# Stage 0 of a transformer layer in token order, with the low-rank products of four tiles at once and the transposes five steps ahead

## What is computed

```
h = layernorm(x)
q = h @ Wq + h @ q_A @ q_B          # rank 16; 16 heads of 128
k = h @ Wk + h @ k_A @ k_B          # 4 heads of 128
v = h @ Wv + h @ v_A @ v_B
q, k = rms_norm, rope, gain (q)
y = causal softmax(q k^T) v,  minus its projection on v
x = x + y @ Wproj + y @ p_A @ p_B
x = x + W_down(silu(W_up h2) * (W_gate h2)),  h2 = layernorm(x), all three weights quantised to -1, 0, 1
```

## Time and profile before

| | us |
|---|---|
| median of 3 runs | 3926.59 |
| the three runs | 3903.36, 3926.59, 4186.11 |
| the profiled execution | 3899.53 |
| its span (slowest core, core 7) | 3898.0 |
| spans of the 8 cores | 3880.8 to 3898.0 |
| PE busy in the span | 3681.1 (94%) |
| DVE, ACT, POOL busy | 1775.4, 930.6, 759.0 |

### The profile page before, as it was taken

One profiled execution on the slowest core, in us unless ns is written; L12 is line 12 of the kernel. 1 busy time (PEld: TensorE's weight loads), 2 busy tenths in 40 slices (PEclk: granted clock), 3 DMA queues, 4 the chain that ended last, 5 costly groups with the idle time before them and its releaser, 6 DMA issues.

```text
span 3898.0 us, 52480 instructions; the slowest of 8 cores (3880.8 to 3898.0 us)
## 1 busy us (share of the span) xinstructions
PE 3681.1 (94%) x19448; PEld 1779.3 (46%) x19448; DVE 1775.4 (46%) x2311; ACT 930.6 (24%) x1658; POOL 759.0 (19%) x900
## 2 busy tenths in 40 slices
PE   6888898948998999999999999999999999999999
PEld 4555554534333444444444444444444444444444
DVE  5667676744346333344433334433333443333343
ACT  4567576744111544200000000000100000101000
POOL 3456666555544000000000000000000000000000
PEclk9999999979999999999999999999999999999999
DMA  6577776696334876546422225632222663222364
GB/s 170 150 217 210 204 219 196 209 207 214 120 118 145 296 283 251 192 173 229 178 77 79 76 76 205 227 141 76 76 76 76 227 229 117 76 76 79 109 230 155
DMA packets 124093, 629.68 MB, mean 162 GB/s; under 512 B 13264, under 2 KB 13584, under 8 KB 73152
## 3 DMA queue, kind: packets, MB, share of 16 engines
q1 hardware_dynamic: 96960, 469.80, 35.1%
q0 software_dynamic: 26880, 156.48, 13.1%
HBM read 555.61 MB, written 92.27 MB: 166 GB/s over the span
## 4 chain that ended last, share of the span: by engine, by line
PE 80%; DMA 7%; DVE 5%; issue 3%; POOL 3%; ACT 1%; DVEq 0%; SPq 0%; POOLq 0%; ACTq 0%
PE accps L1373 67%; PE accps L1177 4%; PE gps L400 4%; DMA pw<-W_gate 3%; DMA pw<-W_up 1%; DMA wq<-Wqkv 1%; PE yps L805 1%; PE sps L772 1%; DVE slabB L1256 1%; DVE ss L440 1%; DVE c L868 1%; DMA yst<-xb 1%; POOL rab L856 1%; DVE pacc L204 1%; DVE slabB L1254 1%
## 5 line engine op out<-in xcount | busy, mean ns | idle before, releaser
L1373 PE MATMUL accps<-slabB,xreg 128*128 128x512 bf16 x8192 | 1775.8, 380 | 3.4 <-DVE slabB L1256 3.4
L1373 PEld LDWEIGHTS accps<-slabB,xreg 128*128 128x128 bf16 x8192 | 803.2, 98 | 975.8 <-issue 16.2
L1373 PE MATMUL accps<-slabA,xreg 128*128 128x512 bf16 x4096 | 884.7, 379 | 0.0
L1386 ACT ACTIVATE xreg<-accps,scl 128x512 f32<-128x512 f32 x256 | 175.6, 688 | 2047.1 <-PE accps L1373 2041.8
L1373 PEld LDWEIGHTS accps<-slabA,xreg 128*128 128x128 bf16 x4096 | 400.8, 98 | 483.3
L1341 DVE TENSOR_SCALAR xreg<-xreg,scl 128x2048 bf16<-128x2048 f32 x192 | 246.6, 1284 | 604.1 <-PE accps L1373 576.2
L1344 DVE SCALAR_TENSOR_TENSOR xreg<-xreg,scl 128x2048 bf16<-128x2048 f32 x192 | 453.1, 2360 | 20.4 <-DVE xreg L1341 0.5
L400 PE MATMUL gps<-wq,slabA 128*128 128x512 bf16 (+1 forms) x2048 | 417.1, 335 | 16.8 <-DMA wq<-Wqkv 14.5
L1400 DVE SCALAR_TENSOR_TENSOR xreg<-accps,scl,xreg 128x512 f32<-128x512 f32 x256 | 192.0, 750 | 471.2 <-PE accps L1373 471.2
L1390 DVE TENSOR_TENSOR slabA<-xreg,accps 128x512 bf16<-128x512 f32 x256 | 175.1, 686 | 504.3 <-PE accps L1373 503.9
L72 POOL DMA_DIRECT2D acc_scr<-xreg x48 | 35.5, 739 | 1559.7 <-DVE xreg L1400 1546.4
(11 more groups left out here) (165 smaller groups left out, 2251.6 us busy)
## 6 DMA issues: line engine op xcount, KB each, us to landing
xreg<-W_down SPq DMA_DIRECT2D x128, 1024.0 KB, 7.8
pw<-W_up SPq DMA_DIRECT2D x128, 512.0 KB, 5.4
pw<-W_gate SPq DMA_DIRECT2D x128, 512.0 KB, 5.5
xreg<-W_up SPq DMA_DIRECT2D x64, 1024.0 KB, 5.2
xreg<-W_gate SPq DMA_DIRECT2D x64, 1024.0 KB, 5.0
xreg<-acc_scr POOLq DMA_DIRECT2D x64, 1024.0 KB, 7.3
acc_scr<-xreg POOLq DMA_DIRECT2D x48, 1024.0 KB, 5.2
outT<-xreg POOLq DMA_DIRECT2D x16, 1024.0 KB, 5.2
```

The source lines that it names most:

```text
L1373: pan_tok[k][tc] = op("tensor", lambda e, tc=tc, dt=dt, mov=mov: e.matmul(bank(st_ + tc), tern[s][:, dt * 128:(dt + 1) * 128], mov, start= ...
L1386: evict[k][tc] = op("scalar", lambda e, tc=tc, cs=cs: e.activation(silu[:, cs], bank(st_ + tc), AF.Silu, scale=scl[:, 1:2]))
```

## The change

Stage 0 takes the tiles in the order 0, 1, 2, ..., 15. Attention and the later groups keep the order TO; `unit_number` gives the place of a unit in either. The low-rank product is made for four tiles at once: `ln_lowrank(b)` in the steps 4, 8, 12 and 16, with 16 matmuls of 512 columns and one copy of 48x512. The q, k, v of tile k-5 (before: of the step k-2) are made in step k, and its finish and transposes are those of tile k-6 (before: of k-3), so the loop has NT + 6 = 22 steps instead of 19. The loads of group 1's weights are issued at step 12 instead of 9, the first piece of W_up in step 8 instead of 5, the sums from step 9 instead of 6.

```
-                    if part == 1 and t == TO[-1]:
+            def unit_number(g, t):
+                return g * NT + TO.index(t) if g else t
+                    if part == 1 and unit_number(g, t) % NT == NT - 1:
...
-            def ln_lowrank(j, toks):
+            def ln_lowrank(b):
                 nonlocal t_free
-                js = slice(TO[j] * 128, (TO[j] + 1) * 128)
-                wait("tensor", *toks)
-                wait("tensor", t_free)
+                js = slice(b * 512, (b + 1) * 512)
+                for j in range(4 * b, 4 * b + 4):
+                    wait("tensor", *ev_tok[j])
+                wait("tensor", t_free, cst)
                 for dt in range(ND):
                     tp = op("tensor", lambda e, dt=dt: e.matmul(
-                        TB[0:48, 0:128], aq[:, dt, :], slabA[:, dt, js],
+                        TB[0:48, :], aq[:, dt, :], slabA[:, dt, js],
                         start=(dt == 0), stop=(dt == ND - 1)), inc=(dt == ND - 1))
                 wait("vector", tp)
-                t_free = xat_tok[TO[j]] = op("vector", lambda e: e.tensor_copy(
-                    xat[:, js], TB[0:48, 0:128]))
+                t_free = op("vector", lambda e: e.tensor_copy(xat[:, js], TB[0:48, :]))
...
-            for k in range(NT + 3):
-                if k == 9:
+            for k in range(NT + 6):
+                if k == 12:
                     for c in range(NCH - 8):
                         load_w(1, c)
                 if 1 <= k <= NT:
                     ev_tok[k - 1] = ln_transpose(k - 1, ln_tok[k - 1])
-                if k >= 3:
-                    unit_finish(k - 3)
+                    xnT_tok[k - 1] = ev_tok[k - 1][0]
+                if k >= 6:
+                    unit_finish(k - 6)
...
-                t = TO[k - 2] if 2 <= k <= NT + 1 else None
+                t = k - 5 if 5 <= k <= NT + 4 else None
...
-                if 1 <= k <= NT:
-                    ln_lowrank(k - 1, ev_tok[k - 1])
+                if 1 <= k <= NT and k % 4 == 0:
+                    ln_lowrank(k // 4 - 1)
...
-                if k >= 3:
-                    unit_transpose(0, TO[k - 3], 2, t_free)
-                    t_free = unit_evict(0, TO[k - 3], 2)
-                if k == 5:
+                if k >= 6:
+                    unit_transpose(0, k - 6, 2, t_free)
+                    t_free = unit_evict(0, k - 6, 2)
+                if k == 8:
                     abs_load(2, *pw_args)
-                elif 5 < k:
+                elif 8 < k:
                     abs_sum("scalar", *pw_args)
```

More of the change, by code:

```diff
@@ L294, in rbank_bf @@
                 return rbank(i).bitcast(BF16)
-            dma("sync", "xs0", xs[0], xb[TO[0] * 128:(TO[0] + 1) * 128, :])
+            dma("sync", "xs0", xs[0], xb[0:128, :])
             dma("gpsimd", "gns", gn[:], gain)
@@ L300, in emit @@
             cst = dma("gpsimd", "cst", aq_h[:, 0:768], a_qkv)
-            dma("sync", "xs1", xs[1], xb[TO[1] * 128:(TO[1] + 1) * 128, 0:1024])
-            dma("sync", "xs1", xs1b, xb[TO[1] * 128:(TO[1] + 1) * 128, 1024:2048])
+            dma("sync", "xs1", xs[1], xb[128:256, 0:1024])
+            dma("sync", "xs1", xs1b, xb[128:256, 1024:2048])
             w_tok = {}
@@ L382, in emit @@
             q_read = {}
+            def unit_number(g, t):
+                return g * NT + TO.index(t) if g else t
             def unit_banks(g, t):
-                u = g * NT + TO.index(t)
+                u = unit_number(g, t)
                 return (2 * u) % 3, (2 * u + 1) % 3
@@ L458, in unit_qk @@
                 nonlocal mq_free
-                s = TO.index(t) % 2
+                s = unit_number(g, t) % 2
                 bq, bk = unit_banks(g, t)
@@ L534, in ln_load @@
                 wait("sync", x_free[s])
-                rows = slice(TO[j] * 128, (TO[j] + 1) * 128)
+                rows = slice(j * 128, (j + 1) * 128)
                 if s == 0:
@@ L587, in ln_transpose @@
                 xnb_free[s] = tp
-                js = slice(TO[j] * 128, (TO[j] + 1) * 128)
+                js = slice(j * 128, (j + 1) * 128)
                 wait("vector", tp)
@@ L596, in ln_transpose @@
                 return m, a
-            def ln_lowrank(j, toks):
+            def ln_lowrank(b):
                 nonlocal t_free
-                js = slice(TO[j] * 128, (TO[j] + 1) * 128)
-                wait("tensor", *toks)
-                wait("tensor", t_free)
+                js = slice(b * 512, (b + 1) * 512)
+                for j in range(4 * b, 4 * b + 4):
+                    wait("tensor", *ev_tok[j])
+                wait("tensor", t_free, cst)
                 for dt in range(ND):
                     tp = op("tensor", lambda e, dt=dt: e.matmul(
-                        TB[0:48, 0:128], aq[:, dt, :], slabA[:, dt, js],
+                        TB[0:48, :], aq[:, dt, :], slabA[:, dt, js],
                         start=(dt == 0), stop=(dt == ND - 1)), inc=(dt == ND - 1))
                 wait("vector", tp)
-                t_free = xat_tok[TO[j]] = op("vector", lambda e: e.tensor_copy(
-                    xat[:, js], TB[0:48, 0:128]))
+                t_free = op("vector", lambda e: e.tensor_copy(xat[:, js], TB[0:48, :]))
+                for j in range(4 * b, 4 * b + 4):
+                    xat_tok[j] = t_free
             ln_tok = {}
@@ L617, in emit, with unit_finish @@
             ABS_0 = NT - 3
-            def unit_finish(j):
-                t = TO[j]
+            def unit_finish(t):
                 unit_ss(0, t)
@@ L638, in emit @@
                         ln_load(k + 2)
-                t = TO[k - 2] if 2 <= k <= NT + 1 else None
+                t = k - 5 if 5 <= k <= NT + 4 else None
                 if t is not None:
-                    xnT_tok[t] = ev_tok[k - 2][0]
-                    wait("tensor", *ev_tok[k - 2])
                     mms = unit_mms(0, t)
```

## The result

The changed kernel takes 3925.18 us (median of 20 runs), the kernel before 3903.38 (median of 20 runs, taken at the same time). The ratio is 1.0053, with a 95% interval from 1.0038 to 1.0068: 0.5% slower, about 20 us, where 18 were forecast. That is within the range of 3899 to 3958 and within the 2% that the forecast gave 96%. The time forecast, 3931, stood on 3913 for the kernel before, and this kernel now takes 3902 to 3905 in the mean. So 18 us on its own mean would have been about 3922: the high base and the 2 to 3 us that the shift was too small cancel in part.

A forecast was written before the change was run, and what follows sets the result against it. PE was busy 94%, and stage 0's end was taken to set the kernel's end: 197.9 us plus 7 of stalls, 205 against 186.85. That is 18 us on 3913, so 3931 us, range 3899 to 3958.

The forecast's parts named there:

- the high base: Time of the kernel before on which the forecast stood: 3913 us, middle of undisturbed times from 3899.5 to 3926.6.
- the shift: Total predicted delay: stage 0, and with it the kernel, ends 18 us later.
- the sum: End of stage 0: 197.9 us without stalls plus 7 of stalls, 205 against 186.85.
- Absorbed: Rival behind stage 0: it ends 18 us later but attention waits less for weights; +0 to +8, 3917; 15%.
- The start: Steps before the first unit: tiles 3 and 4 normed first at 6.2 us a step, first product 5.4, step 5 at 57.1.
- The short and the long steps: Steady part of stage 0: eight steps without a product at 8.2 us, three with one at 10.9.
- one loop, through the shift: Clean steps: transposes, DVE copy, finish, DVE's shift and ACT's norm hold a step at 8.1 us even if PE is free.
- The 0.2 for DVE's statistics: Long steps: DVE's statistics behind the copy of the product add 0.2 us to PE's 10.7, making 10.9.
- The end: Last steps of stage 0, without layernorm: four together 28.5 us, then a last one of 6.98.
- The stalls: Late loads of weights, W_up and x in stage 0: 7 us in all, bounds 1 and 13.
- PE's work decides: Rival for stage 0, the faster side: short steps take PE's 7.2 us; 3910 on the forecast's scale; 15%.
- Worse stalls: Rival for stage 0: loads meet in fewer steps and the clock falls; stalls 13 to 25 us, 3945 to 3955; 15%.

The follow-up runs named there:

- order: The kernel before with only the token order changed to 0 to 15; stage 0 ends at 184.4 us, ratio to before 1.0003.
- lead5_single: The changed kernel, lead of five kept, with one low-rank product for each tile again; stage 0 ends at 199.9 us, ratio to before 1.0035.
- earlynorm_after: The changed kernel with inverse root, shift and norm moved ahead of scaling and rotation; stage 0 ends at 200.5 us, ratio to before 1.0050.
- late_transpose: earlynorm_after with the transposes of q and k one step later; stage 0 ends at 197.3 us, ratio to before 1.0029.
- load7: The changed kernel with group 1's first four weight pieces loaded at step 7 instead of 12; stage 0 ends at 200.9 us, ratio to before 1.0043.
- load18: The changed kernel with group 1's first four weight pieces loaded at step 18 instead of 12; stage 0 ends at 202.9 us, no ratio given.

## Why the prediction was right

**The question and the scale.** That a microsecond at the end of stage 0 is one at the end of the kernel was the base of the sum; 19.9 us there and 20 to 21 in the spans show it. *Absorbed* fell: the wait behind stage 0 was 22.83 us after 22.66. The mechanism of the sum held too: the loss lies in half-filled steps and long steps, not in PE's work. But two of its terms came near by errors that cancel.

**The start: near by luck.** Step 5 was forecast at 57.1 us (bounds 55.2 and 58.6); it began between 54.9 and 56.3 on the 8 cores, 55.5 in the mean. The path there was another. The timeline of the changed kernel, core 1:

```profile
35.74 2.37 ACT L577 ACTIVATE pring<-pw,mv 128x1024 bf16<-128x1024 f32 x2 [0.41 <-DVE mv L569]
...
40.41 2.47 DVE L554 BATCH_NORM_STATS2 st<-yst 128x6 f32<-128x512 f32 x4 [4.82 <-DMA yst<-xb]
...
46.91 2.47 DVE L554 BATCH_NORM_STATS2 st<-pw 128x6 f32<-128x512 f32 x4 [2.65 <-DMA pw<-xb]
```

The prediction said "the norm of tile 2 ends at 42.3 as before"; it ended at 38.1: DVE's pause of 2.5 to 3.3 us behind the statistics of tile 2, read in before, order and lead5_single, isn't there, and why stays open. Against that, tiles 3 and 4 were late, while the prediction said "the DMA queues don't stand in the way", from a stretch that begins at 47.37, when group 0's weights had landed. So step 3 took 8.5 us in the mean instead of 6.2. In lead5_single, where the norm of tile 2 ends at 42.2, the steps with layernorm alone take 6.4, as forecast. The first product was forecast at 5.4 us with the clock turning within it and took 5.3 in the mean. What I hadn't seen is that this product does the warming that the first unit would otherwise pay for: step 5 takes 7.3 us in the changed kernel and 9.9 in lead5_single.

**The short and the long steps.** Forecast 8.2 and 10.9, measured 8.1 to 8.2 and 10.7. The number of the short step was right and its reason only half so: I named one loop, through the shift, and took PE's 7.2 as the next bound. There were two loops, and cutting the first left 8.0 (earlynorm_after); with the second cut as well it is 7.5 (late_transpose). The 0.2 for DVE's statistics behind the copy of the product isn't in the long step, which is all PE's, but in the one behind it, and it is more: 8.7 us, 0.5 over a clean step (0.8 in load7 and load18).

**The end.** 7.12 us for each of the four steps, measured 6.95.

**The stalls: the size right, the working not.** 7 us forecast, bounds 1 and 13. On core 1 the step from 126.82 alone is 10.4 over a clean one, on the mean of the cores 7.5. I took 5.5 us for W_up less the 2.7 that the long step covers, and 2.7 for the x tile behind it. The piece was that of step 12, as said, and the long step gave it some cover (step 13 is 1.0 us shorter than in lead5_single). But it wasn't as late as before: it took 15.9 us from its issue instead of 11.8. The x tile behind it, on the other hand, cost next to nothing, since ACT's wait covered it (DVE waits for it on one of the 8 cores, 0.27 us, and on two others for the tile after it, up to 0.88). Two wrong terms again give about the right sum.

**The rivals.** *PE's work decides* was wrong for the changed kernel, and so is the rule on larger matmuls of "Perfetto Trace Analysis" in the Trainium skill as far as time goes: at a lead of five, products of four tiles cost 4.1 us. *Worse stalls* fell in the mean of the cores: the short steps from 6 to 15 hold 8.7 us over 8.2 each. On the slowest core they hold 12, near this rival's 13, and the granted clock did fall there. Its price of 3945 to 3955 doesn't follow from its own terms either: stalls of 13 to 25 us in place of 7 are 3937 to 3949. "Most of the loss lies" in the half-filled steps: the lead costs 15.5 of 19.9 us, 20.8 at the end less what the start gives back.

## What to carry to other kernels

Work taken from the busiest engine is worth nothing in a step that two loops through the other engines hold at the same length; look at which wait stands next behind the first, and cut it too before counting on the gain. Gathering small products into one big one makes steps uneven, and where buffers keep the steps in lockstep the long ones cost in full and the short ones save nothing. A longer lead in a software pipeline whose engines run in order gives no slack in its middle; it costs a half-filled step at the end for each step of lead, and gives back only as far as there is an idle wait at the start for it to fill. A forecast can be right by terms that cancel: each term is to be checked against its own row.

## What was unexpected of the hardware

The same 16 transposes take 1.86 us at the start of lead5_single and 1.07 us in the changed kernel, because 5 us of a low-rank product had been run before them: PE work placed in an idle stretch ahead of the main work is repaid by the clock, here with 2.3 us at the start of step 6.

Loads that are issued in a burst (four weight pieces) delay a neighbour wherever they are put, whether this neighbour is x or W_up. The longest wait of ACT or DVE for such a load was, from core to core, 5.6 to 7.8 us at step 4, 2.0 to 5.1 at step 7, 3.6 to 6.3 at step 9, 4.2 to 9.4 at step 12 and 2.7 to 7.0 at step 18.
